# A gated delta-rule layer on one core: the levels of its triangular inverse on 64 columns instead of 128

## The reference, cut to what matters

```
M = -tril(einsum('bhnik,bhnjk->bhnij', k_beta, k) * decay, k=-1)
T = solve_triangular(eye - M, eye, lower=True)
v_new      = T @ v_beta
k_cumdecay = T @ (k_beta * exp(g))
# then a scan over the chunks of a sequence carries a 128 x 128 state
```

## Time and profile before

| | |
|---|---|
| median of three runs | 5981.18 us |
| profiled execution: its span, which is its own time here | 5983.6 us |
| PE busy | 5351.0 us, 89% |
| DVE busy | 4743.2 us, 79% |
| ACT busy | 4155.5 us, 69% |
| POOL busy | 3081.8 us, 52% |

### The profile page before, as it was taken

One profiled execution on the slowest core, in us unless ns is written; L12 is line 12 of the kernel. 1 busy time (PEld: TensorE's weight loads), 2 busy tenths in 40 slices (PEclk: granted clock), 3 DMA queues, 4 the chain that ended last, 5 costly groups with the idle time before them and its releaser, 6 DMA issues. The chain is left out here.

```text
span 5983.6 us, 146544 instructions
## 1 busy us (share of the span) xinstructions
PE 5351.0 (89%) x45450; PEld 4415.7 (74%) x45578; DVE 4743.2 (79%) x8288; ACT 4155.5 (69%) x10963; POOL 3081.8 (52%) x3690
## 2 busy tenths in 40 slices
PE   2899999999999999999999999999999999999867
PEld 2677777777777777777777777777777777777756
DVE  4788888888888888888888888888888888888754
ACT  1677777777777777777777777777777777777634
POOL 0555555555555555555555555555555555555434
PEclk8999999999999999999999999999999999999988
DMA  3010101010101010100101010101010101010000
GB/s 105 31 36 27 36 27 36 27 36 27 36 27 36 27 36 27 36 27 30 32 27 36 27 36 27 36 27 36 27 36 27 36 27 36 27 36 27 18 29 21
DMA packets 130814, 194.64 MB, mean 33 GB/s; under 512 B 13344, under 2 KB 61600, under 8 KB 130464
## 3 DMA queue, kind: packets, MB, share of 16 engines
q1 hardware_dynamic: 129312, 190.78, 10.0%
q10 hardware_dynamic: 1152, 0.79, 0.1%
HBM read 185.75 MB, written 5.77 MB: 32 GB/s over the span
## 5 line engine op out<-in xcount | busy, mean ns | idle before, releaser
L865 DVE CAST_PREDICATED pl<-masks,pa 128x512 f16<-128x512 uint16 x1536 | 983.6, 683 | 84.3 <-PE pa L593 84.2
L771 ACT ACTIVATE u<-pa 128x512 f16<-128x512 f32 x1536 | 924.5, 602 | 16.2 <-PE pa L607 8.2
L824 DVE SCALAR_TENSOR_TENSOR conv<-pb,cws,conv 128x511 f32<-128x511 f32 (+2 forms) x1152 | 831.5, 740 | 65.6 <-ACT conv L714 65.6
L1001 POOL TENSOR_TENSOR xo<-xo,zs 128x512 f32<-128x512 f32 x256 | 327.5, 1279 | 745.1 <-DVE xo L923 745.1
L516 PE MATMUL pb<-xb,wb 128*128 128x512 f32 x2304 | 626.6, 407 | 1.7 <-POOL xb L995 1.7
L603 PE MATMUL pa<-pl,u 128*128 128x128 f16 x6144 | 602.7, 221 | 3.0 <-DVE pl L865 3.0
L607 PE MATMUL pa<-u,pl 128*128 128x128 f16 x6144 | 595.1, 219 | 0.0
L779 ACT ACTIVATE yb<-pb 128x256 f32<-128x256 f32 x512 | 196.7, 384 | 531.2 <-PE pb L647 372.5
L593 PE MATMUL pa<-t,a 128*128 128x128 f16 x6144 | 495.4, 220 | 73.7 <-DVE t L858 72.8
L870 DVE CAST t<-pa 128x512 f16<-128x512 f32 x768 | 527.1, 686 | 1.7 <-PE pa L603 1.3
L593 PEld LDWEIGHTS pa<-t,a 128*128 128x128 f16 x6144 | 388.3, 98 | 189.8 <-DVE attn L838 48.3
(11 more groups left out here) (171 smaller groups left out, 13882.1 us busy)
## 6 DMA issues: line engine op xcount, KB each, us to landing
tokn<-in_Wqkvz SPq DMA_DIRECT2D x256, 256.0 KB, 2.7
conv<-in_xT SPq DMA_DIRECT2D x256, 256.0 KB, 3.3
conv<-in_Wqkvz SPq DMA_DIRECT2D x128, 256.0 KB, 2.8
gxb<-in_xT SPq DMA_DIRECT2D x8, 512.0 KB, 3.6
wout<-in_W_out SPq DMA_DIRECT2D x1, 4096.0 KB, 17.7
yacc<-in_x_tok SPq DMA_DIRECT2D x2, 2048.0 KB, 20.6
out<-fob SPq DMA_DIRECT2D x8, 512.0 KB, 2.9
lrow<-rows_scratch SPq DMA_DIRECT2D x128, 6.0 KB
```

The lines of the kernel that those rows point to most:

```text
L771: nc.scalar.activation(group(u16_, g), four(pa[2 * g]), ACT.Copy).then_inc(u_ready[g].sem, 1)
L824: nc.vector.scalar_tensor_tensor(out=conv[c][:, back:S], in0=proj_bank[c][:, 0:S - back], scalar=cws[p][:, c * TAPS + 3 - back:c * TAPS + ...
L865: nc.vector.copy_predicated(group(pl[l], g), masks[:, l:l + 1, :].broadcast_to([128, 4, C]), four(pa[2 * g + 1])).then_inc(p_ready.sem, 1)
```

## The change: what it does

At level l only the first s of every 2s columns of `pl` and T can change, and only the last s of every 2s columns of U. The change makes every matmul and copy of a level touch these 64 of a unit's 128 columns alone. The moving operand of a matmul becomes a strided view with runs of s columns (2 at level 0, 64 at level 5); its result is written densely, 64 columns per unit. The copies read the dense 256 elements and write them to the strided view; P takes the first half of the bank `pa[2g+1]`, and T the second half. The weights stay 128 x 128. The number of instructions, their order and their semaphores are as before.

```diff
--- before.py
+++ after.py
@@ -362,6 +362,22 @@
 
             return t[:, 4 * g:4 * g + 4, :]
 
+        def halves(t, g, l, odd):
+
+            return group(t, g).rearrange("p u (b w s) -> p u b w s", w=2, s=2 << l)[:, :, :, odd, :]
+
+        def half_unit(t, u, l, odd):
+
+            return t[:, u, :].rearrange("p (b w s) -> p b w s", w=2, s=2 << l)[:, :, odd, :]
+
+        def packed(bank, at, l):
+
+            return bank[:, at:at + 2 * C].rearrange("p (u b s) -> p u b s", u=4, s=2 << l)
+
+        def packed_unit(bank, at, u):
+
+            return bank[:, at + u * (C // 2):at + (u + 1) * (C // 2)]
+
         def per_head(x):
 
             return x[:, :, None, :].broadcast_to([128, 2, R, C])
@@ -590,8 +606,8 @@
                     if l == 0 and g == 1:
                         pe.wait_ge(vt_ready.sem, vt_ready.at(a, 1))
                     for u in range(4):
-                        last = nc.tensor.matmul(pa[2 * g + 1][:, u * C:(u + 1) * C], a16[:, 4 * g + u, :],
-                                                t16_[:, 4 * g + u, :], start=True, stop=True)
+                        last = nc.tensor.matmul(packed_unit(pa[2 * g + 1], 0, u), a16[:, 4 * g + u, :],
+                                                half_unit(t16_, 4 * g + u, l, 0), start=True, stop=True)
                     last.then_inc(p_mm.sem, 1)
 
             def ut_product(a, p, i):
@@ -600,11 +616,11 @@
                 if l:
                     pe.wait_ge(u_ready[g].sem, u_ready[g].at(a, l))
                 for u in range(4):
-                    last = nc.tensor.matmul(pa[2 * g + 1][:, u * C:(u + 1) * C], u16_[:, 4 * g + u, :],
-                                            pl[l][:, 4 * g + u, :], start=True, stop=True)
+                    last = nc.tensor.matmul(packed_unit(pa[2 * g + 1], 2 * C, u), u16_[:, 4 * g + u, :],
+                                            half_unit(pl[l], 4 * g + u, l, 0), start=True, stop=True)
                 last.then_inc(t_mm.sem, 1)
                 for u in range(4):
-                    last = nc.tensor.matmul(pa[2 * g][:, u * C:(u + 1) * C], pl[l][:, 4 * g + u, :], u16_[:, 4 * g + u, :],
+                    last = nc.tensor.matmul(packed_unit(pa[2 * g], 0, u), pl[l][:, 4 * g + u, :], half_unit(u16_, 4 * g + u, l, 1),
                                             start=True, stop=True)
                 last.then_inc(u_mm.sem, 1)
 
@@ -765,10 +781,10 @@
                 for g in range(2):
                     if g == 1:
                         act.wait_ge(t_mm.sem, t_mm.at(a, 2 * l + 2))
-                        nc.scalar.activation(group(t16_, g), four(pa[2 * g + 1]), ACT.Copy)\
+                        nc.scalar.activation(halves(t16_, g, l, 0), packed(pa[2 * g + 1], 2 * C, l), ACT.Copy)\
                             .then_inc(t_ready[g].sem, 1)
                     act.wait_ge(u_mm.sem, u_mm.at(a, 2 * l + g + 1))
-                    nc.scalar.activation(group(u16_, g), four(pa[2 * g]), ACT.Copy).then_inc(u_ready[g].sem, 1)
+                    nc.scalar.activation(halves(u16_, g, l, 1), packed(pa[2 * g], 0, l), ACT.Copy).then_inc(u_ready[g].sem, 1)
 
             def y_copy(b, p, n):
                 act.wait_ge(y_mm.sem, y_mm.at(b, n + 1))
@@ -862,12 +878,13 @@
                 for g in range(2):
                     ve.wait_ge(p_mm.sem, p_mm.at(a, 2 * l + g + 1))
                     ve.sem_inc(passed[0].sem, 1)
-                    nc.vector.copy_predicated(group(pl[l], g), masks[:, l:l + 1, :].broadcast_to([128, 4, C]),
-                                              four(pa[2 * g + 1])).then_inc(p_ready.sem, 1)
+                    mask = masks[:, l, :].rearrange("p (b w s) -> p b w s", w=2, s=2 << l)[:, :, 0, :]
+                    nc.vector.copy_predicated(halves(pl[l], g, l, 0), mask[:, None, :, :].broadcast_to([128, 4, C // (4 << l), 2 << l]),
+                                              packed(pa[2 * g + 1], 0, l)).then_inc(p_ready.sem, 1)
 
             def ut(a, p, l):
                 ve.wait_ge(t_mm.sem, t_mm.at(a, 2 * l + 1))
-                nc.vector.tensor_copy(group(t16_, 0), four(pa[1])).then_inc(t_ready[0].sem, 1)
+                nc.vector.tensor_copy(halves(t16_, 0, l, 0), packed(pa[1], 2 * C, l)).then_inc(t_ready[0].sem, 1)
 
             def resid(a, p, g):
                 ve.wait_ge(resid_mm.sem, resid_mm.at(a, g + 1))
```

## The result

The kernel after took 6023.83 us (median of 4 runs, 6013.91 to 6025.1), the kernel before 5983.61 (4 runs, 5980.92 to 5990.64). The ratio is 1.0058 with an interval of 1.0046 to 1.0070: some 0.6% slower, by more than the 0.2% that can be told from no change. Forecast were 5829 us and, in the range, 5800 to 5948. The profiled execution has a span of 6023.2 us, where the sum gave 5831.6.

What follows compares the result with a forecast made beforehand. The prediction took TensorE as the limit in part of the levels and chains across engines or VectorE elsewhere. Savings of 1.19 us a step times 128 gave 152 us off 5983.6, 5831.6 profiled, median 5829 us; range 5800 to 5948.

Steps and rivals of the forecast that it cites:

- Prices: Unit costs in the levels: VectorE copies 0.42 us, ScalarE copies 0.38, four 64-column matmuls 0.12 instead of 0.225.
- Rival (a): Level matmuls: 128-column weights hold the pace, so 64 columns also take 0.055 us; 5944 us, chance 0.14.
- rival (c): Strided views in the levels: each run costs a restart, so slower, 6211 us at 8 ns a run; chance 0.06.
- Levels 0 and 1: First two levels of a step: fewer matmul columns save 0.21 us each, so keys_state behind level 1 starts 0.42 earlier.
- Levels 2 and 3: Level 2's chain of 4.08 us stands and q_part in level 3 hangs on its end; 0.0 us saved.
- the term of 0.29: Level 4: shorter predicated copies let o_norm start 0.71 us earlier, 0.29 of it saved here.
- Its 1.36 us stay: Level 4: o_norm keeps its duration of 1.36 us beside GpSimd's long operation.
- Level 5 and the last copy: Level 5's eight p_product matmuls save 0.21 us; the last copy of T, opening VectorE's stretch behind the levels, 0.27.
- Sum of a clean step: Whole step: 0.21 + 0.21 + 0.29 + 0.21 + 0.27 = 1.19 us saved, taken for all 128 steps.
- others: Remaining cases, such as a stretch in which the clock falls; chance 0.05, no time given.
- 128 like steps: Nearly the whole span: 128 equal steps of 42.94 us each, 5496 of 5983.6 us.

Runs made afterwards that it cites:

- g0wide_ord: g0wide with o_norm moved behind level 4's copies, o_turn behind the projection of Q, x_copy behind its tap; 5809.29 us, 0.9705 of the kernel before.
- fill24: Kernel after plus 24 unused 128-column matmuls ahead of the first update_product of every second step; 5902.72 us, 0.9864 of the kernel before.
- g0wide: Kernel after, but level 0's matmuls ahead of the wait for y_copy stream 128 columns again, copies stay narrow; 5873.57 us, 0.9803 of the kernel before.
- wide0: Kernel before with the change in levels 1 to 5 alone, level 0 left as it was; 5887.31 us, 0.9841 of the kernel before.
- late_yb3: Kernel before with three extra chained ScalarE copies of yb ahead of the first y_copy of every second step; 6168.03 us, 1.0298 of the kernel before.
- late_yb: Kernel before with one extra ScalarE copy of yb ahead of the first y_copy of every second step; 6025.75 us, 1.0055 of the kernel before.
- only0: Kernel before with the whole change in level 0 alone, levels 1 to 5 left as they were; 6197.36 us, 1.0363 of the kernel before.
- fill8: Kernel after plus 8 unused 128-column matmuls ahead of the first update_product of every second step; 5923.87 us, 0.9879 of the kernel before.

## Why the prediction was wrong

The timeline of a clean step of the kernel after carries the first points:

```profile
3086.45 0.70 PE L647 MATMUL pb<-st,kq 128*128 128x256 f32 x2
...
3090.45 0.70 PE L647 MATMUL pb<-st,kq 128*128 128x256 f32 x2
3094.45 1.02 POOL L1025 TENSOR_TENSOR rr<-rse,expo_eps 128x4 f32<-128x4 f32 x1
3094.70 0.75 DVE L882 CAST_PREDICATED pl<-masks,pa 128x256 f16<-128x256 uint16 x2
3095.44 1.29 POOL L1018 TENSOR_TENSOR xo<-xo,zs 128x512 f32<-128x512 f32 x1
3095.50 1.77 DVE L946 TENSOR_TENSOR xo<-xo,rr 128x512 f32<-128x512 f32 x1
...
3095.86 0.29 PE L619 MATMUL pa<-pl,u 128*128 128x64 f16 x4
3095.98 0.28 PE L623 MATMUL pa<-u,pl 128*128 128x64 f16 x4
...
3097.41 0.65 PE L702 MATMUL pb<-ident,xo 128*128 128x128 f32 x4 [0.91 <-DVE xo L946]
3105.34 0.68 DVE L946 TENSOR_TENSOR xo<-xo,rr 128x512 f32<-128x512 f32 x1
```

and GpSimd's long operation at that place of the kernel before:

```profile
3077.72 1.28 POOL L1001 TENSOR_TENSOR xo<-xo,zs 128x512 f32<-128x512 f32 x1
```

1. **Prices: right.** 421, 387 and 420 ns for the copies, and 3095.86 to 3095.98 for four matmuls, the 0.12 of the forecast; four of them last 0.28, as it said. Rival (a) falls with that, and with it, for these loads, the Trainium skill's rule for the weight load ("TensorE: Matmul & The Clock Gate", section "LDWEIGHTS (loading the stationary operand)"), by which, as an estimate (four loads of 107 ns), they would be 0.43 apart. A load of these is recorded at 98 to 101 ns in the mean, near that rule; but one starts every 0.03 us, so the loads overlap and their time doesn't set the pace. The pair of predicated copies takes 0.76 us at level 0 (runs of 2 columns) and 0.75 at level 4 (runs of 32), so rival (c) isn't there.
2. **Levels 0 and 1: right in clean steps.** Counted from the step's first residual, `keys_state` behind level 1 starts 0.38 us earlier than before; forecast was 0.42.
3. **Levels 2 and 3: right.** From `keys_state` to `keys_state` the chain takes 3090.45 - 3086.45 = 4.00 us (4.08 in the earlier trace rows), and `q_part` starts 0.38 earlier, no more.
4. **Level 4: the term of 0.29 was mis-sized, it is 0.0.** `o_norm` does start 0.78 us earlier, about as forecast (0.71). But "Its 1.36 us stay" was wrong: it takes 1.77. The same operation takes 0.68 where GpSimd is idle (3105.34). In the earlier trace rows it ran from 3078.18, beside GpSimd's long operation that had begun at 3077.72; now both begin together, 3095.44 and 3095.50, and overlap for 1.23 us instead of some 0.8. In both kernels `o_norm` ends 0.54 us behind the end of GpSimd's operation (3079.54 against 3079.00, 3097.27 against 3096.73), and within 0.01 of it in 127 of 128 steps; its own start doesn't matter there. GpSimd's operation ends 0.37 us earlier, so the transposes are earlier by 0.37 only, as everything ahead of them already was. `g0wide_ord` tests this: there `o_norm` starts 0.17 us before GpSimd's operation ends and takes 0.72, which is 0.55 behind that end again.
5. **Level 5 and the last copy: right.** 0.2 and 0.27 us, and the rest of the step follows.
6. **Sum of a clean step:** 0.88 us instead of 1.19. Over 128 steps that is 40 of the 192 us by which the sum missed the profiled execution.
7. **Loop-end steps: the step that failed.** The prediction put it so: "Levels 0 and 1 of every second step wait longer for `y_copy`; their saving lies behind that wait and is the same." It saw the wait and the lengthening, and took the clock of the earlier trace rows as given; a falling clock stood among the "others" with 0.05, without a price. The prediction's "128 like steps" hid that every second one has this wait. The matmuls ahead of it got short, the wait grew from 1.13 to 1.54 us (median 1.18 to 1.42), and the clock fell in 61 of these steps. With 0.88 saved they would be 42.89 us long; they are 45.4, so 64 x 2.5 = 160 us. The two terms give 200 for the 192 missing. The price per fall can be read too: loop-end steps of 44.3 us have 3.4 us at half clock, those of 46.9 have 10.2, so against some 42.8 us without a fall (`fill24`, `g0wide`) a fall costs 1.5 to 4.1 us.

That the falls cause the loss, and don't only go with it, rests on `fill24`, `wide0` and `g0wide`: three different edits that keep the clock up in most loop-end steps, each of which brings the loop-end step to 43.0. That a gap in TensorE's work alone can lower the clock rests on `late_yb3`; that in this change it took the narrow matmuls ahead of the gap rests on `g0wide`, `wide0` and `late_yb`. In the kernel after the clock fell 0.6 to 1.5 us behind the start of the wait, in `late_yb3` 1.6 to 3.2, and in half of the loop-end steps of `only0` before its start. So what TensorE did before counts, the shorter waits and the narrow `p_product` at the start of a step included. Which of them weighs how much is not settled. Why `only0`, with less taken out, falls more often and longer than the kernel after, and why falls in clean steps are 1 in the kernel after but 12 and 21 in `fill24` and `fill8`, is open.

The Trainium skill has a section on this behaviour ("TensorE: Matmul & The Clock Gate", section "HAM oscillation — how this bites in real kernels"), where the re-throttling is told of a kernel that waits for its DMAs each pass; the section behind it ("A second HAM failure mode: psum-queue depth-cycling") tells it of one that idles briefly between groups of matmuls. The traces here agree in kind: 62 falls, once a loop body. In the kernel after they lie at waits of 1.1 to 1.8 us for another engine's copy.

## What to carry to other kernels

When a change takes work off TensorE, don't only ask which work was on the path: list TensorE's idle stretches that lie behind the removed work, and price a fall of the clock there (here 1.5 to 4.1 us each, 62 times, against 0.88 us a step gained). If the clock gives way in the trace after, give back the removed columns just ahead of that wait alone: 16 of 144 matmuls were enough, and turned 0.6% slower into 2.0% faster. An operation whose time is stretched by a neighbour has no fixed duration: `o_norm` ended 0.54 us behind GpSimd's operation wherever it began, so starting it earlier gave nothing; starting it as the neighbour ends cost nothing.

## What the runs showed of the hardware that I had not expected

- The stretches at half clock inside the loop came in three lengths, 3.4, 6.8 and 10.2 us, and in no other, in all kernels of the table.
- Waits of TensorE of 1.1 to 1.3 us went with a fall of its clock 37 times in 37 behind narrow matmuls (the kernel after, `only0`), and once in 108 behind wide ones (before, `wide0`, `g0wide`).
- VectorE's 128 x 512 operation of two operands from SBUF took 0.68 us alone, 1.36 with some 0.8 us of GpSimd's long operation beside it, and 1.77 with 1.23 us. In the kernels before, after and `g0wide_ord` it ended 0.54 to 0.55 us behind the end of GpSimd's operation in nearly every step in which the two overlapped (127 of 128 in the first two), however early it had begun.
- At the end of a two-step loop body ScalarE stood for "issue", 2.5 to 3.0 us in nine of ten steps before and after. Behind a body of four steps TensorE stood too, up to 5.2 us, and the end cost 5.5 us instead of 1.5.
- Runs of 2 half-precision values cost next to nothing: a pair of predicated copies took 0.76 us at level 0 and 0.74 to 0.75 with runs of 8 to 32, four matmuls 0.28 us at either, and a copy 423 ns with a strided read and write, 421 with a strided write only.
